# A transformer layer with mixture-of-experts on one core: block diagonals on ScalarE, an early input norm, and new hand-written orders

## The reference

```python
x = x + xattn(layernorm(x), ctx)   # a = attention(xn, xn) causal, + xn; layer norm with gamma, beta
                                   # c = attention(h, ctx) + h;  norm;  relu(h W1 + b1) + h;  norm;  relu
x = x + attn(layernorm(x))         # 16 heads of 32, causal softmax, weights times a decay matrix, W_proj
x = x + ffn(layernorm(x))          # silu(x sw1) * (x sw2), layer norm, sw3; 1024 rows also pass
                                   # a gate and the best of 8 experts
return x
```

## Time and profile before

| | |
|---|---|
| median of 3 runs | 1449.03 us (1448.67 to 1449.30) |
| the profiled execution | span 1452.8 us; no other time of its own is given |
| TensorE busy | 1365.6 us, 94% |
| VectorE busy | 1128.1 us, 78% |
| ScalarE busy | 601.9 us, 41% |
| GpSimd busy | 526.1 us, 36% |
| mean granted TensorE clock | 0.988 of full speed |
| transfers | 201.41 MB, 139 GB/s on average |

### The profile page before, as it was taken

One profiled execution on the slowest core, in us unless ns is written; L12 is line 12 of the kernel. 1 busy time (PEld: TensorE's weight loads), 2 busy tenths in 40 slices (PEclk: granted clock), 3 DMA queues, 4 the chain that ended last, 5 costly groups with the idle time before them and its releaser, 6 DMA issues.

```text
span 1452.8 us, 33270 instructions
## 1 busy us (share of the span) xinstructions
PE 1365.6 (94%) x13860; PEld 851.7 (59%) x13861; DVE 1128.1 (78%) x2335; ACT 601.9 (41%) x1147; POOL 526.1 (36%) x545
## 2 busy tenths in 40 slices
PE   7679999999999999999999999999999999998888
PEld 3355566666656666665665656666665666655443
DVE  6787777777787877778778877777778877777776
ACT  2544444443444444343434444444444444443222
POOL 0133333433444333443443333343443433343222
PEclk9899999999999999999999999999999999999899
DMA  9732444433333444433333344443333344434440
GB/s 349 259 131 74 146 146 146 144 123 105 133 112 115 146 146 146 146 137 101 122 130 105 139 146 146 146 142 114 111 138 105 123 146 146 147 134 161 149 161 30
DMA packets 38662, 201.41 MB, mean 139 GB/s; under 512 B 5096, under 2 KB 5992, under 8 KB 28400
## 3 DMA queue, kind: packets, MB, share of 16 engines
q1 hardware_dynamic: 37648, 198.93, 38.3%
q10 hardware_dynamic: 864, 0.36, 0.1%
HBM read 182.24 MB, written 17.04 MB: 137 GB/s over the span
## 4 chain that ended last, share of the span: by engine, by line
PE 70%; DVE 19%; POOL 4%; ACT 4%; issue 3%; DMA 0%; DVEq 0%; POOLq 0%; ACTq 0%; SPq 0%
PE ps_a L1716 11%; PE ps_a L1739 8%; PE ps_t L1739 7%; PE ps_t L1703 6%; PE ps_a L1725 6%; PE ps_a L1751 4%; PE ps_a L1783 4%; POOL rstd L636 4%; PE ps_t L1716 3%; PE ps_v L1716 3%; DVE stats L1178 3%; DVE arena L1309 3%; PE ps_t L1826 2%; PE ps_t L1775 2%; PE ps_t L1751 2%
## 5 line engine op out<-in xcount | busy, mean ns | idle before, releaser
L645 POOL TENSOR_TENSOR act_l<-act_t,act_h 128x512 f16<-128x512 f32 (+1 forms) x176 | 199.5, 1134 | 351.4 <-ACT act_t L789 199.4
L636 POOL TENSOR_TENSOR rstd<-var,mhalf 128x1 f32<-128x1 f32 x224 | 181.8, 812 | 333.7 <-DVE var L1180 328.9
L781 ACT ACTIVATE act_h<-ps_t,scale 128x512 f16<-128x512 f32 (+1 forms) x110 | 70.8, 644 | 206.2 <-PE ps_t L1703 206.2
L645 POOL TENSOR_TENSOR last_slot<-last_slot 128x512 f16<-128x512 f32 x80 | 90.0, 1125 | 156.7 <-ACT last_slot L789 90.8
L1739 PE MATMUL ps_a<-act_h,arena 128*128 128x128 f16 x1408 | 87.6, 221 | 17.3 <-ACT act_h L781 17.3
L1739 PEld LDWEIGHTS ps_a<-act_h,arena 128*128 128x128 f16 x1408 | 81.9, 99 | 28.3 <-ACT act_h L781 21.3
L789 ACT ACTIVATE act_t<-ps_t,scale 128x512 f32<-128x512 f32 (+1 forms) x110 | 70.3, 639 | 49.1 <-PE ps_t L1703 49.1
L1739 PE MATMUL ps_t<-act_h,arena 128*128 128x128 f16 x1408 | 87.0, 221 | 3.3 <-ACT act_h L781 3.3
L1716 PE MATMUL ps_a<-arena,act_h 128*128 128x512 f16 x352 | 83.6, 380 | 1.9 <-ACT act_h L781 1.9
L1309 DVE TENSOR_SCALAR arena<-ps_a,unscale 32x512 f32<-32x512 f32 x64 | 48.2, 753 | 47.0 <-PE ps_a L1751 45.8
L1739 PEld LDWEIGHTS ps_t<-act_h,arena 128*128 128x128 f16 x1408 | 81.4, 99 | 4.9 <-DVE arena L1037 2.4
(11 more groups left out here) (380 smaller groups left out, 3150.7 us busy)
## 6 DMA issues: line engine op xcount, KB each, us to landing
arena<-in_ctx_t SPq DMA_DIRECT2D x32, 2056.0 KB, 8.4
arena<-in_ctx_n SPq DMA_DIRECT2D x32, 2048.0 KB
ctx_last<-in_ctx_last SPq DMA_DIRECT2D x32, 256.0 KB
arena<-in_ew SPq DMA_DIRECT2D x8, 1024.0 KB, 6.3
x_in<-in_x SPq DMA_DIRECT2D x22, 256.0 KB, 7.3
x_scratch<-rows SPq DMA_DIRECT2D x22, 256.0 KB, 8.8
out<-rows SPq DMA_DIRECT2D x22, 256.0 KB, 2.1
arena<-in_ew SPq DMA_DIRECT2D x8, 512.0 KB, 7.2
```

The lines of the kernel that those rows point to most:

```text
L636: nc.gpsimd.tensor_tensor(rstd[s][:], var[s][:], mhalf[:], ALU.pow).then_inc(rstd_ready[s], 1)
L645: nc.gpsimd.tensor_tensor(act_l[s][:, chunks], act_t[s][:, chunks], act_h[s][:, chunks], ALU.subtract).then_inc(act_l_ready[s], 1)
L781: nc.scalar.activation(act_h[s][:, 0:width // P].rearrange("p c r -> p (c r)"), bank[s][:, 0:width], ACT.Copy, scale=scale[:, k:k + 1]).th ...
```

## The change

Six things change.

- The orders FIRST, ORDER and LAST are all new. A round now begins at another unit, so most lags differ by one from before. The parts that matter for a steady round are in the diff.
- turn_p moves from TensorE and ScalarE to VectorE, as a transpose of 32x32 blocks. This gives the whole transpose, as only the blocks on the diagonal are not zero.
- All four key blocks are written by ScalarE (`key_blocks`, in two units). The head weights get one VectorE transpose of 128x512 in place, and ScalarE copies it to the block diagonals in four passes of 32x512 (`weight_blocks`). Both arrays have a new layout, with the block index outermost: the source and target of a copy are contiguous, and a product reads its 128 columns as four pieces of 32.
- The moments of the input x have buffers and semaphores of their own (`x_stats`, `x_mv`, `x_var`, `x_rstd`), so they can be made while the slot's other buffers are in use.
- `chain.last` increments without waiting; the unit that needs the step waits by `made_by`. The scale of the scores goes into `unscale`, and `reduce_max(..., negate=True)` replaces a maximum and a multiplication.
- b3 is added to x2 on GpSimd in a new unit `x2_bias`, and ffn_out on VectorE becomes one pass instead of two.

```diff
 ORDER = {
+    "pe": [(2, "context_out"), (1, "self_scores"), (3, "project_v_l"), (2, "context_out_l"), (1, "value_self"),
+        (1, "value_self_l"), (3, "head_mix"), (1, "self_mix"), (2, "turn_h2"), (3, "project_out"),
+        (3, "project_out_l"), (2, "hidden"), (2, "hidden_l"), (1, "turn_h"), (3, "turn_x2n"),
+        (1, "project_query"), (1, "project_query_l"), (3, "ffn_in"), (1, "context_scores"), (3, "ffn_in_l"),
+        (1, "turn_pc"), (2, "turn_x1n"), (1, "context_mix"), (2, "project_k"), (2, "project_q"), (3, "turn_z"),
+        (2, "project_k_l"), (2, "project_q_l"), (3, "ffn_out"), (3, "ffn_out_l"), (0, "turn_xn"),
+        (2, "project_v"), (2, "head_scores"), (1, "turn_w"), (0, "project_self"), (0, "project_self_l")],
+    "dve": [(4, "z_norm"), (2, "context_total"), (4, "ffn_out"), (2, "context_scaled"), (3, "head_scores"),
+        (3, "head_total"), (1, "project_self"), (3, "head_weights"), (1, "self_scores"), (2, "context_out"),
+        (1, "turn_p"), (2, "context_norm"), (0, "xn_moments"), (1, "self_mix"), (3, "project_out"),
+        (1, "self_norm"), (3, "x2_norm"), (2, "hidden"), (2, "out_norm"), (1, "context_scores"), (2, "x1_norm"),
+        (3, "ffn_in"), (3, "silu"), (0, "turn_xn"), (1, "context_mix")],
...
+    "pool": [(4, "x2_bias"), (1, "turn_xn"), (2, "turn_w"), (3, "head_scores"), (2, "context_out"), (3, "head_mix"),
+        (1, "self_mix"), (0, "xn_moments"), (2, "turn_h2"), (3, "project_out"), (1, "turn_h"), (2, "hidden"),
+        (3, "turn_x2n"), (2, "out_norm"), (2, "turn_x1n"), (3, "silu"), (3, "turn_z")],
...
-            kbd = ....rearrange("p (c g h k) -> p c g h k", c=C, g=G, h=HPC)
-            pbd = ....rearrange("p (h g q) -> p h g q", h=NH, g=G)
+            kbd = ....rearrange("p (h c g k) -> p h c g k", c=C, g=G, h=HPC)
+            pbd = ....rearrange("p (g h q) -> p g h q", h=NH, g=G)
...
+                def x2_bias(s, r, tile):                                    # GpSimd
+                    pool.wait_ge(rows_ready[s], 5 * r + 4)
+                    pool.wait_ge(x2_stored[s], 16 * r + 32)
...
+                    nc.gpsimd.tensor_tensor(rows3[s][:], rows3[s][:], b3[:], ALU.add).then_inc(x2_biased, 1)
...
+                        for h in heads:                                     # ScalarE, key_blocks
+                            mine = slice(HD * h, HD * (h + 1))
+                            nc.scalar.activation(kbd[mine, h, :, :, :].rearrange("p c g k -> p (c g k)"),
+                                                 ps_a[s][mine, :], ACT.Copy,
+                                                 scale=unscale[mine, K_WATTN:K_WATTN + 1]).then_inc(k_ready, 1)
...
+                        for g in groups:                                    # ScalarE, weight_blocks
+                            mine = slice(T * g, T * (g + 1))
+                            nc.scalar.copy(pbd[mine, g, :, :].rearrange("p h q -> p (h q)"), rows3[s][mine, :]
+                                           ).then_inc(pbd_ready, 1)
...
+                def turn_p(s, r, tile):                                     # VectorE
+                    chain = Chain("turn_p", s, r)
+                    dve.wait_ge(p_ready[s], 3 * r + 1)
+                    nc.vector.transpose(p_t[s][:, 0:P], p_n[s][:, 0:P]).then_inc(p_t_ready[s], 1)
+                    chain.last(nc.vector.reciprocal(inv[s][:, 0:1], total[s][:, 0:1]))
...
                     chain(nc.vector.tensor_tensor(by_head(rows1[s][:]), sc, per_head(inv[s][:]), ALU.mult))
-                    for g in range(G):                                      # head_weights
-                        rows = slice(T * g, T * (g + 1))
-                        nc.vector.transpose(pbd[rows, :, g, :], by_head(rows1[s][rows, :])).then_inc(pbd_ready[s], 1)
+                    nc.vector.transpose(sc, by_head(rows1[s][:])).then_inc(heads_turned, 1)
...
-                    chain(nc.vector.scalar_tensor_tensor(rows2[s][:], ps_a[s][:], unscale[:, K_W3:K_W3 + 1], b3[:],
-                                                         ALU.mult, ALU.add))
-                    nc.vector.tensor_tensor(rows2[s][:], rows2[s][:], rows3[s][:], ALU.add).then_inc(out_ready[s], 1)
+                    dve.wait_ge(x2_biased, tile + 1)                        # ffn_out
+                    nc.vector.scalar_tensor_tensor(rows2[s][:], ps_a[s][:], unscale[:, K_W3:K_W3 + 1], rows3[s][:],
+                                                   ALU.mult, ALU.add).then_inc(out_ready[s], 1)
...
-                                                  kbd[:, c, g, :, :].rearrange("p h k -> p (h k)"),
+                                                  kbd[:, :, c, g, :],       # TensorE, head_scores
...
-                                                  pbd[:, head, :, :].rearrange("p g q -> p (g q)"),
+                                                  pbd[:, :, head, :],       # TensorE, head_mix
```

More of the change, by code:

```diff
@@ L75 @@
 FIRST = {
[L76 to L85, removed]
@@ L103 @@
-    "pool": [(2, "set_2"), (3, "turn_z"), (0, "xn_moments"), (1, "set_1"), (0, "turn_xn"), (2, "head_scores"),
-        (1, "turn_w"), (2, "head_mix"), (1, "context_out"), (1, "turn_h2"), (2, "project_out"), (0, "self_mix"),
-        (0, "turn_h"), (1, "hidden"), (2, "turn_x2n"), (1, "out_norm"), (1, "turn_x1n"), (2, "silu")],
+    "pe": [(2, "context_out"), (1, "set_09"), (1, "set_10"), (2, "set_21"), (2, "context_out_l"), (0, "set_01"),
+        (1, "value_self"), (0, "set_02"), (1, "set_11"), (1, "self_scores"), (1, "value_self_l"),
+        (3, "project_v_l"), (2, "turn_h2"), (1, "self_mix"), (2, "hidden"), (0, "set_03"), (2, "hidden_l"),
+        (3, "head_mix"), (1, "turn_h"), (3, "project_out"), (0, "set_04"), (3, "project_out_l"), (0, "set_05"),
+        (1, "project_query"), (1, "project_query_l"), (0, "set_06"), (3, "turn_x2n"), (3, "set_22"),
+        (1, "context_scores"), (1, "set_12"), (3, "ffn_in"), (1, "turn_pc"), (2, "turn_x1n"), (3, "ffn_in_l"),
+        (3, "set_23"), (1, "set_13"), (2, "project_k"), (2, "project_q"), (2, "project_k_l"),
+        (2, "project_q_l"), (0, "set_07"), (3, "turn_z"), (1, "context_mix"), (3, "ffn_out"), (3, "ffn_out_l"),
+        (0, "turn_xn"), (2, "head_scores"), (0, "project_self"), (1, "turn_w"), (2, "project_v"), (0, "set_08"),
+        (0, "project_self_l")],
@@ L106 @@
+    "pool": [(4, "x2_bias"), (1, "turn_xn"), (3, "head_scores"), (2, "turn_w"), (2, "set_1"), (2, "context_out"),
+        (2, "turn_h2"), (1, "self_mix"), (3, "head_mix"), (1, "turn_h"), (3, "project_out"), (2, "hidden"),
+        (3, "turn_x2n"), (2, "out_norm"), (2, "turn_x1n"), (0, "xn_moments"), (2, "set_2"), (3, "silu"),
+        (3, "turn_z")],
 }
 ORDER = {
-    "pe": [(2, "project_q"), (3, "turn_z"), (2, "project_k_l"), (3, "ffn_out"), (3, "ffn_out_l"), (1, "turn_pc"),
-        (2, "project_q_l"), (1, "context_mix"), (2, "head_scores"), (0, "turn_xn"), (2, "project_v"),
-        (0, "project_self"), (0, "project_self_l"), (1, "turn_w"), (2, "project_v_l"), (1, "context_out"),
-        (0, "self_scores"), (1, "context_out_l"), (0, "value_self"), (0, "value_self_l"), (0, "turn_p"),
-        (2, "head_mix"), (0, "self_mix"), (2, "project_out"), (1, "turn_h2"), (2, "project_out_l"), (1, "hidden"),
-        (1, "hidden_l"), (0, "turn_h"), (2, "turn_x2n"), (0, "project_query"), (0, "project_query_l"), (2, "ffn_in"),
-        (0, "context_scores"), (2, "ffn_in_l"), (1, "turn_x1n"), (1, "project_k")],
@@ L160 @@
+    "pool": [(3, "out_norm"), (3, "turn_x1n"), (4, "silu"), (4, "e_zn2"), (1, "xn_moments"), (4, "turn_z"), (3, "e_zn0"),
+        (4, "x2_bias"), (1, "turn_xn"), (2, "turn_w"), (3, "head_scores"), (3, "e_zn1"), (2, "e_norm"),
+        (2, "context_out"), (3, "head_mix"), (1, "self_mix"), (2, "turn_h2"), (3, "project_out"), (1, "turn_h"),
+        (4, "e_zn3"), (2, "hidden"), (3, "turn_x2n")],
 }
@@ L1766, in self_scores @@
                     mm.then_inc(scored[s], 1)
-                def turn_p(s, r, tile):
-                    pe.wait_ge(p_ready[s], 3 * r + 1)
-                    nc.tensor.transpose(ps_a[s][:, 0:P], p_n[s][:, 0:P], ident[:]).then_inc(p_turned[s], 1)
                 def self_mix(s, r, tile):
```

316 lines of the change are left out of this document (160 added, 156 removed), and 10 rows, old and new, of the table FIRST.

## The result

The changed kernel takes 1425.38 us in the median (1424.66 to 1430.97, 4 runs) against 1449.09 (4 runs) for the one before: a ratio of 0.9842, 95% interval 0.9824 to 0.9860. The forecast was 1433 and faster. The profiled execution of the changed kernel has a span of 1423.8 us, 29.0 under the 1452.8 of the earlier trace rows. That is more than the 23.7 between the medians, since the profiled execution of the kernel before was a long one: in the 49 other executions on record its span was 1446.6 to 1450.5 us, while the changed kernel's other spans were 1422.9 to 1429.2.

The account below looks back on a forecast made before the run. TensorE, 94% busy, sets the pace. Terms took a round from 40.64 to 40.19 us: -14 over 31 intervals, -3 early, span 1436, and 1433 us after 0.26% off for the runs; own range 1422 to 1443.

Parts of the forecast that it names:

- Step 2: TensorE order around project_k: its 0.94 us wait goes, turn_pc waits 0.42 and context_mix 0.19 per round.
- Step 1: turn_p leaves TensorE: -0.20 us per round; VectorE's 128x128 transpose in its place takes 0.25 and fits.
- Step 3: GpSimd's queue around project_out_l to turn_x2n: hidden_l 0.6 us late, +0.37 at project_query, -0.29 from remainder waits per round.
- the 0.75: From project_out_l to turn_x2n TensorE has 0.75 us too little work per round; this was to stay.
- the +0.37: project_query waits 0.37 us more per round, as late hidden_l makes turn_h and ScalarE's pass behind it late.
- The -0.29: Waits for GpSimd's remainder go: 0.14 us at project_query_l and 0.15 at ffn_out per round.
- Step 4: Block diagonals: ScalarE's copies hidden before head_mix, one 128x512 transpose 0.70 us, reading in four pieces costs 0.
- the cover of 0.4: ScalarE's copies of the head weights end at 6.3, 0.4 us before head_mix is due at 6.7.
- Steps 5 and 6: ffn_out's second pass and b3 on GpSimd, x moments' own buffers, unwaited chains, folded scales, SyncE's unchanged loads: nothing.
- "More": Rival, chance 0.16: the 0.98 us of added waits isn't there, rounds take 39.2 and the time is 1402.
- "The form fails": Rival, chance 0.08: half-speed strided reading (+2.1 per round) or a 2.8 us transpose (about +0.8): 1457 to 1498.
- "Slower": Rival, chance 0.17: GpSimd's turn_h2 remainder holds self_norm on VectorE by 0.82 us; rounds of 41.0, time 1460.

Follow-up runs that it names:

- The second and third run with the old LAST: Kernel before plus the change's parts in old orders, b3 on VectorE: 1481.18 us; then the same with project_k2 behind turn_pc on ScalarE: 1453.11 us.
- the last experiment: Changed kernel with context_scores' exponential sum on VectorE, xn_moments behind out_norm, and self_norm ahead of project_out on VectorE: 1454.79 us, ratio 1.0026 to the kernel before.

## Why the prediction came out as it did

**What was right.** The direction, the time but for 7.6 us, and the structure: a round of 39.92 against 40.19, most of the gain in the steady rounds, TensorE's waits named. Starts on TensorE, in both kernels, split the 0.71 of a round as follows, by step:

| stretch | forecast | measured |
|---|---|---|
| project_k's wait gone, turn_pc and context_mix waiting (2) | -0.94 + 0.42 + 0.19 = -0.33 | -0.24 |
| turn_p gone (1), everything from ffn_out_l on to head_mix | -0.20 | -0.16 |
| head_mix to project_query (3) | +0.37 | -0.05 |
| waits for GpSimd's remainders behind it (3) | -0.29 | -0.26 |
| sum | -0.45 | -0.71 |

- Step 2. turn_pc comes 0.35 late (from ffn_in_l to it 1.22 for 0.87; forecast 0.42) and context_mix 0.17 late (0.62 for 0.45; forecast 0.19). The whole is 0.09 short, since turn_pc and context_mix are 0.05 and 0.12 longer from start to start than before. The swap behind it is worth 0.85 when undone.
- Step 1. turn_p took 0.20 from start to start before, as I put it, and all of it is gone. The 128x128 transpose takes 0.31 on VectorE (forecast 0.25), hidden. The other +0.04 of the row are small shifts: head_mix starts 0.96 behind value_self_l for 0.86 of work (+0.10), and the rest gives 0.06 back.
- Step 3, the term that was mis-sized. The order in GpSimd's queue was right, hidden_l is late, and the 0.75 stayed: from project_out_l to turn_x2n it is 4.67, for 0.87 + 1.73 + 0.87 + 0.45 = 3.92 of work. But I put hidden_l 0.6 late and it is 0.19 late. In the kernel before it was 0.15 late already (1.88 from hidden to hidden_l), which I had not seen. VectorE's self_mix pass began 2.28 behind head_mix's start, at 8.98 in the layout, where I had 9.3, since I reckoned some 0.3 too much for what lies ahead of it. GpSimd's three operations then took 2.63 from the start of the first to the end of the last, and not 2.75. With 0.41 less delay turn_h ends early enough, ScalarE has its block ready (577.91) when turn_x2n is done (project_query starts at 578.01), and the +0.37 at project_query falls to nothing: 1.48 lie from turn_h to project_query in both kernels. That one term explains 0.42 of a difference of 0.26; the other three were each 0.03 to 0.09 too hopeful. The run with xn_moments moved shows that even the 0.19 lies in shadow.
- The -0.29 is -0.26, but I put 0.14 of it at project_query_l by the durations in the earlier trace rows. By starts that product set takes 0.90 in both kernels; the 0.10 was at project_q_l, and 0.16 at ffn_out.
- Step 4. One transpose of 128x512 takes as long as one of 32x512, and reading in pieces is free (32 head_mix products take 1.01 again). By form and line, after:

```profile
L866 ACT ACTIVATE arena<-ps_a,unscale 32x512 f32<-32x512 f32 x128 | 86.4, 675 | 11.0 <-PE ps_a L1784 7.8
...
L880 ACT COPY arena<-rows 32x512 f32<-32x512 f32 x88 | 53.8, 612 | 3.8 <-DVE rows L1377 2.2
...
L675 POOL TENSOR_TENSOR rows<-rows,b 128x512 f32<-128x512 f32 x22 | 28.1, 1275 | 2.9 <-DMA x_scratch<-rows 2.7
...
L1377 DVE STREAM_TRANSPOSE rows<-rows 128x512 f32<-128x512 f32 x22 | 15.6, 711 | 0.8
...
L1268 DVE STREAM_TRANSPOSE p_t<-p_n 128x128 f32<-128x128 f32 x32 | 10.0, 311 | 7.0 <-ACT p_n L840 7.0
```

  The four copies took 2.52 us together where I had 2.2; in the layout's positions they ran from 3.94 to 6.46, and I had 4.1 to 6.3. Most of the cover of 0.4 was used up: the last copy ends 0.24 ahead of head_mix, which itself starts 0.96 behind value_self_l, for 0.86 of work. The 0.10 that head_mix is late isn't theirs, since it is there too in the run with the blocks on VectorE, where ScalarE copies nothing; its cause stays open.
- Steps 5 and 6 were nothing, as forecast; VectorE has 27.7 a round (28 forecast) and ScalarE 21.4 (20.5).
- The early rounds gave 2.9 (forecast 3). No run separates FIRST, so what in it gave them isn't shown.
- The end gave 8.6 by the profiles, where I had 2.7 (six intervals of 0.45) and nothing beside, with bounds of +10 and -12. I didn't lay LAST out. Not all of the 8.6 is the change's: of the 23.7 between the medians, 17.5 are in the steady rounds and 2.9 ahead of them, which leaves about 3 for the end (an estimate, since it mixes medians with profiles). The last four rounds take 159.2 us (40.39, 40.39, 39.86, 38.60) and not 174.8 (41.33, 43.61, 49.62, 40.26), and what lies behind the last head_mix takes 56.7 and not 49.8. The second and third run with the old LAST have slow late rounds as before (44.89, 49.38, 48.82 and 41.12 in the third), so what gain there is goes with the new LAST. How large it is, and which of its swaps brings it, stays open.

So by the medians the forecast's 16 us were 23.7. In the 25 steady rounds they were 17.5 for 11.3, and these 6 us are shown; the other 1 to 2 aren't placed. (1436 less 0.26% is 1432 and not 1433; it changes nothing.) That the time came within 8 us owes something to luck: the +0.37 that wasn't there is larger than the whole error of a round, and three other terms, each too hopeful by 0.03 to 0.09, made up for part of it.

**The rivals.** "More" was wrong in size (39.2) and partly right in kind: one of the added waits wasn't there. "The form fails" is excluded by the rows above. "Slower" didn't happen in this order of work, but the last experiment shows that it was near: there xn's power no longer lies between self_mix's power and the remainder, and the swap of self_norm brings the meeting. The swap alone, with xn's power still in between, wasn't run. In the changed kernel self_norm starts 0.14 behind the end of the remainder (575.58 to 575.72), since project_out's pass and moments stand ahead of it. The pass at L1231, over the whole changed kernel, and then in the last experiment:

```profile
L1231 DVE SCALAR_TENSOR_TENSOR rows<-rows,rstd,beta x66: 725/751/753, 53.3 to 1343.5; 128x512 f32<-128x512 f32 x66
```

```profile
L1231 DVE SCALAR_TENSOR_TENSOR rows<-rows,rstd,beta x66: 726/751/1636, 54.6 to 1373.1; 128x512 f32<-128x512 f32 x66
```

In the kernel before, the same pass had reached 1567, but only twice, at 140.06 and 183.73, both in the slow rounds ahead of the steady ones; after, not one of 66 is held. So in steady rounds neither kernel has a two-input pass of 1.5 us, and the new orders keep what the old ones had. They don't keep all meetings out: the powers take 0.99 to 1.01 in place of 0.55 as a rule, and at x2 that is in the 0.33 that turn_x2n waits. In one round, of 40.19, the power got in first, took 0.55, and self_norm started 0.28 late. In another, of 40.11, head_scores' subtraction (L1361) lasts 1.22 in place of 0.69. Two more lines of the changed kernel show what I had overlooked:

```profile
L1226 DVE SCALAR_TENSOR_TENSOR v_n<-v_n,mv,ln_g x22: 475/916/916, 151.2 to 1382.6; 128x256 f32<-128x256 f32 x22
...
L1339 DVE SCALAR_TENSOR_TENSOR rows<-rows,x_in x22: 691/692/1704, 99.8 to 1344.3; 128x512 f32<-128x512 f32 x22
```

silu's scaling (L1226, 128x256) starts while a remainder of GpSimd is running and takes 0.92 in the median, where it took 0.62 before (L1187); no engine is listed as waiting for it. out_norm's last pass (L1339) is held three times, at 1221.52, 1261.91 and 1302.30, once in each of the first three late rounds, and takes 1.70 in place of 0.69. Each time it starts at the same moment as one of GpSimd's remainders (L657). These three rounds take 40.39, 40.39 and 39.86; what the meeting costs them wasn't measured by itself.

## What to carry to other kernels

Lay the round out in start-to-start intervals and put the slack into the places where one result has to pass two other engines: one swap in TensorE's list was worth 0.85 us a round, and each of three misplaced units of mine cost between 1 and 10 us a round. Work taken from an engine with air bought nothing by itself here (b3); it can buy freedom for the order, so plan the two together. A delay under the shadow of a longer chain is worth nothing either: before you shorten a wait, ask which chain ends last behind it, and when one semaphore frees two engines that can hold each other, look at what each of them does next.
